# Second layer's routing cut into small pieces between the mixer's steps, with fixed regions per expert in the sorted rows

## The chip, the cores and the metric

One NeuronCore of a Trainium2 chip runs one program. Its engines are TensorE (PE in the profile), VectorE (DVE), ScalarE (ACT), GpSimd (POOL) and SyncE (SP), which issues most of the DMAs. The metric is the device time of one execution in microseconds, less is better.

## The reference, cut to what matters

Two transformer-like layers work on x of 4 groups (batch entries) of 512 rows of 256 features. Layer 0 is an attention and a mixture of 16 experts (top 2), layer 1 a state-space mixer and a mixture of 32 experts (top 6) with a shared expert. The change touches the mixer and the second mixture:

```
h = _layernorm(x, axis=-1) * (1 + cb) + sb
x = x + gb * _L1_ffn_ref(h, ...)
# _L1_ffn_ref, HID = 256, N_EXP = 32, F_EXP = 96, TOP_K = 6, F_SH = 192
scores = jax.nn.sigmoid(x @ gate_w)
topk_w, topk_i = jax.lax.top_k(scores, TOP_K)
topk_w = topk_w / (jnp.sum(topk_w, axis=-1, keepdims=True) + 1e-20)
combine = jnp.sum(jax.nn.one_hot(topk_i, N_EXP, dtype=topk_w.dtype) * topk_w[..., None], axis=1)
g = jnp.einsum('td,edf->tef', x, wg)
u = jnp.einsum('td,edf->tef', x, wu)
act = jax.nn.silu(g) * u
routed = jnp.einsum('tef,efd,te->td', act, wd, combine)
shared = jax.nn.silu(hidden_states @ sg) * (hidden_states @ su) @ sd
return routed + shared
```

The mixer (`ssm_forward`) works on each group alone, so a group's x is final for the second mixture as soon as the mixer has finished that group.

## The kernel before, in words

The program runs four stages in order: attention, `experts(0)`, the mixer, `experts(1)`. Between stages all engines meet (`together`).

**The mixer.** After a start part it runs a stream of steps, 32 per group (`FT`), one for each pair of heads, software-pipelined over five steps (`tiles[0]` to `tiles[4]` in `mixer_pe_step`, `mixer_act_step`, `mixer_dve_step`, `mixer_pool_step`). `mixer_stream` writes four steps of a group out in line, then `between` (the tail of the group before: its rows are scaled, gated and added to x), then a hardware loop (`Fori`) of seven turns of four steps. Each engine executes its part of a step in written order and waits on the others by semaphores. PE: projection of x (L1752), transposes (L1766), the products of a chunk (L1775, L1780), projection of the gate (L1752), chunk states (L1792, L1799), output projection (L1806). DVE: states `st` (L1887, L1892), `m_mat` (L1939, into `outs`), `xdt` (L1904), three conv taps `cv` (L1914), `yd`, `xc`, `sgt` (L1921 to L1933). POOL: `xdec` (L1966), a sum of squares (L1974), `yg` (L1981). SP loads `wi`, `l_mat`, `wo`, 1.1 MB in each step.

**The second mixture** (`experts(1)`). Rows are handled in 16 tiles of 128 (`NT`). First comes the routing of all 16 at once: DVE takes the statistics of the layer norm (L1146), normalizes (L1159), PE turns (L949), ACT modulates into `ht`, PE makes the logits (L959), ACT and DVE the sigmoid (L1080, L1177, L1178), DVE the top 8 and their indices (L1181, L1185), the one-hot tables `eqs` (L1190) and their sum `mask` (L1194). PE counts, with a triangular matrix, each row's rank within its expert, and each expert's rows. DVE then knows how many tiles of 128 each expert takes (L1207 to L1217), adds the expert's first row and picks for each row and choice the place in `sorted_rows` (L1219 to L1221). POOL scatters the rows there by 96 indirect DMAs of 128 rows (L1134), each row with its weight and its destination in two further words (L1128, L1129). SP has meanwhile loaded the weights (L920 to L925) and waits for all scatters before it loads the first sorted tile (L931).

Then 143 units run in a pipeline: 16 units of the shared expert, which read `ht` and need no scatter, and 127 tiles of `sorted_rows` (`Q1`). A unit is: turn (L997), gate and up product (L1007 or L1013, the expert's number read from `te` into a register, L1010), tanh (L1099), silu (L1229, L1234), turn (L1023 to L1026), down product (L1038 or L1042), scaling (L1106), and an indirect DMA of 128 rows into `chosen_rows` (L1138). Eight tile buffers (`xt`): a load waits for the put of the tile eight before. At the end SP loads the chosen rows group by group (L937), and PE and DVE add the six.

## Time and profile before

| | us |
|---|---|
| median of 3 runs | 2503.9 (2501.62 to 2505.82) |
| the profiled execution | 2514.42 |
| its span | 2512.6 |
| mean granted PE clock | 0.889 of full |
| busy: PE, DVE, ACT, POOL | 2006.3, 1661.3, 1451.7, 901.4 |

Everything below is read on the profiled execution's axis, from 0 to 2512.6. The stages: attention to 629.6, the first mixture to 862.6, the mixer's start to 988, its stream to 2044 and its last tail to 2051.2, then the second mixture: routing, scatters and shared units to 2243.7, routed units to 2461.7, the adding of the chosen rows to the end. A line number such as L1134 is one of the kernel before. Times of a row are its start and its duration; the bracket at its end is how long its engine had been idle and what released it ("remote" and "issue" mean that no instruction of another engine in the profile explains the end of the wait).

### The profile page before, as it was taken

To read this page: it belongs to the slowest core of one execution; us is meant where nothing else is said; L and a number is where in the kernel's file an instruction comes from. 1 tells how busy PE (TensorE), PEld (TensorE's weight loads), DVE (VectorE), ACT (ScalarE), POOL (GpSimd) and SP (SyncE) were. 2 spreads that over 40 slices of the span, in tenths; PEclk is the share of its full clock that TensorE was granted. 3 is DMA by queue.
4 is the path that set the end of the run, shared out by engine and by line. 5 is a ranking of instruction groups with operands and counts; after the bars stand their busy time and mean duration, and the time that the engine had idled before them with its cause. 6 is when DMAs were issued, how large, how long until landed. Compare 5 with 4: busy or idle time off the path is not lost.

```text
span 2512.6 us, 45894 instructions
## 1 busy us (share of the span) xinstructions
PE 2006.3 (80%) x12171; PEld 1623.7 (65%) x12171; DVE 1661.3 (66%) x3638; ACT 1451.7 (58%) x3953; POOL 901.4 (36%) x832
## 2 busy tenths in 40 slices
PE   4786858777369446999999999999999975259995
PEld 4565646666347244888878887888788863147772
DVE  4665746566424577888888888888888866034444
ACT  1463726456124155888878888888888851015551
POOL 0120302011243110444444444444444434745551
PEclk8796969779679778999999999999999987579998
DMA  3160582011433302444434443444344434225556
GB/s 121 43 192 8 166 229 101 34 67 64 191 98 108 143 5 85 141 150 144 150 121 150 147 148 126 144 150 150 124 143 148 150 104 123 101 90 157 157 154 259
DMA packets 155925, 319.51 MB, mean 127 GB/s; under 512 B 20177, under 2 KB 93905, under 8 KB 153489
## 3 DMA queue, kind: packets, MB, share of 16 engines
q1 hardware_dynamic: 141296, 278.31, 34.7%
q0 software_dynamic: 14496, 39.73, 4.4%
q8 instruction: 47, 0.77, 0.1%
q14 instruction: 86, 0.70, 0.1%
HBM read 231.68 MB, written 86.29 MB: 127 GB/s over the span
## 4 chain that ended last, share of the span: by engine, by line
PE 60%; DVE 12%; issue 10%; ACT 9%; DMA 2%; POOL 2%; PEldq 1%; SPq 1%; DVEq 1%; ACTq 1%; PEld 1%; POOLq 0%
PE bank L1752 14%; PE bank L1806 8%; PE bank L1013 6%; PE bank L1780 5%; ACT work L669 4%; PE bank L1042 3%; PE bank L1799 3%; PE bank L1792 3%; PE bank L1766 3%; DVE nmax L589 2%; PE bank L1775 2%; PE bank L997 1%; PE bank L741 1%; PEldq L142 1%; POOL sorted_rows L1134 1%
## 5 line engine op out<-in xcount | busy, mean ns | idle before, releaser
L1752 PE MATMUL bank<-h_hi,wi 128*128 128x512 f32 x1024 | 402.1, 434 | 0.9 <-ACTq L142 0.9
L1914 DVE SCALAR_TENSOR_TENSOR cv<-bank,cw,cv 128x511 f32<-128x511 f32 (+2 forms) x384 | 287.4, 748 | 83.6 <-ACT cv L1847 50.6
L1841 ACT ACTIVATE l_mat<-l_mat,cum_tok 128x128 f32<-128x128 f32 x1024 | 315.7, 429 | 0.0
L1966 POOL TENSOR_TENSOR xdec<-xdt,dec_tok 128x384 f32<-128x384 f32 x128 | 107.8, 842 | 464.4 <-DVE xdt L1904 464.4
L1981 POOL TENSOR_TENSOR yg<-yd,sgt 128x512 f32<-128x512 f32 x128 | 228.2, 1783 | 76.1 <-DVE yd L1921 76.1
L1806 PE MATMUL bank<-wo,yg 128*128 128x256 f32 x1024 | 242.4, 380 | 0.3 <-POOL yg L1981 0.3
L1138 POOL DMA_INDIRECT chosen_rows<-experts_yo,experts_xt x174 | 167.7, 964 | 192.3 <-ACT experts_yo L1106 169.8
L1229 DVE SCALAR_TENSOR_TENSOR experts_sg<-experts_th,bank 128x96 f32<-128x96 f32 (+2 forms) x190 | 53.8, 283 | 274.8 <-ACT experts_th L1099 206.4
L1752 PEld LDWEIGHTS bank<-h_hi,wi 128*128 128x128 f32 x1024 | 194.4, 190 | 62.2 <-issue 24.2
L1752 PE MATMUL bank<-h_lo,wi 128*128 128x512 f32 x512 | 202.9, 396 | 0.0
L1099 ACT ACTIVATE experts_th<-bank 128x96 f32<-128x96 f32 (+2 forms) x190 | 52.0, 273 | 256.9 <-remote 116.8
L1806 PEld LDWEIGHTS bank<-wo,yg 128*128 128x128 f32 x1024 | 184.9, 191 | 20.5 <-POOL yg L1981 0.7
L1974 POOL TENSOR_TENSOR gates<-gates,sq 128x512 f32<-128x512 f32 x128 | 163.2, 1275 | 92.4 <-ACT sq L1857 92.4
L1013 PE MATMUL bank<-experts_wgu,experts_xT 128*128 x696 | 177.6, 378 | 8.4 <-issue 5.8
L808 POOL CAST w_hi<-w_raw 128x512 fp32r<-128x512 f32 x32 | 19.5, 610 | 452.1 <-ACTq L142 314.8
L1862 ACT ACTIVATE thx<-cv 128x512 f32<-128x512 f32 x128 | 80.7, 631 | 166.9 <-DVE cv L1914 166.9
L1832 ACT ACTIVATE y_off<-bank,e_tok 128x64 f32<-128x64 f32 x768 | 170.1, 327 | 6.1 <-PE bank L1799 6.1
L669 ACT ACTIVATE work<-bank,nmax 128x512 f32<-128x512 f32 (+3 forms) x256 | 135.1, 535 | 65.0 <-DVE nmax L589 65.0
L1939 DVE TENSOR_TENSOR outs<-l_mat,g_mat 128x1024 f32<-128x1024 f32 x128 | 156.6, 1224 | 0.0
L589 DVE TENSOR_REDUCE nmax<-bank 128x1 f32<-128x512 f32 (+3 forms) x256 | 117.5, 483 | 57.9 <-PE bank L746 57.9
L627 DVE TENSOR_TENSOR hb<-bank,pt_hi 128x512 fp32r<-128x512 f32 (+1 forms) x192 | 114.4, 599 | 47.2 <-ACT pt_hi L622 47.1
L1134 POOL DMA_INDIRECT sorted_rows<-experts_rows,slot_u x128 | 125.3, 979 | 55.7 <-issue 36.1
(296 smaller groups left out, 4898.8 us busy)
## 6 DMA issues: line engine op xcount, KB each, us to landing
wi<-in_weights_split SPq DMA_DIRECT2D x128, 512.0 KB, 3.4
l_mat<-running_sums SPq DMA_DIRECT2D x128, 512.0 KB, 4.5
experts_xt<-sorted_rows SPq DMA_DIRECT2D x174, 129.0 KB
experts_got<-chosen_rows SPq DMA_DIRECT2D x32, 512.0 KB, 9.9
wo<-out_weights_normed SPq DMA_DIRECT2D x128, 128.0 KB, 2.0
sorted_rows<-blank SPq DMA_DIRECT2D x5, 2709.0 KB, 26.7
w_raw<-in_wi SPq DMA_DIRECT2D x32, 256.0 KB, 2.6
in_weights_split<-w_hi SPq DMA_DIRECT2D x32, 256.0 KB, 2.8
```

The costliest lines, as they stand in the source:

```text
L589: last = e.tensor_reduce(nmax[:, h, q:q + 1], bank[n % 3][:, col:col + P * (q + 1)], AX.X, ALU.max, negate=True)
L669: last = e.activation(pp[:, h % 2, QOFF[q]:QOFF[q] + w], bank[u][:, col:col + w], ACT.Exp, bias=nmax[:, h, q:q + 1], accum_out=ssum[:, h, ...
L1013: mm = e.matmul(B_G[n % 2][:, 0:2 * F], xT[:, q % TURNED, k, :], wgu[:, bass.ds(owners[q], 1), k, :], start=(k == 0), stop=(k == KD - 1))
L1138: e.indirect_dma_start(chosen[layer], bass.IndirectOffsetOnAxis(xt[:, q % LOADED, D + 1:D + 2].bitcast(U32), 0), yo[:, q % YIELDED, :], No ...
L1752: mm = e.matmul(dst[:, :], l, r[:, k, tok], start=(n == 0), stop=(n == 3 * KD - 1))
L1806: mm = e.matmul(token_major((bank[0], bank[1]), i), yg[:, w.two, i * P:(i + 1) * P], wo[:, w.two, :], start=False, stop=w.end, skip_group_ ...
L1832: last = e.activation(y_off[:, c, rows], PO[:, c * P + hh * SSM_P:c * P + (hh + 1) * SSM_P], ACT.Identity, scale=e_tok[:, c, hh, bass.ds(w ...
L1841: last = e.activation(part, part, ACT.Relu, bias=cum_tok[:, c, hh, bass.ds(w.g, 1)], scale=-1.0)
L1914: e.scalar_tensor_tensor(out=cv[:, w.two, n:SEQ], in0=PSX[w.two][:, 0:SEQ - n], scalar=cw[:, bass.ds(w.f, 1), TAPS - 1 - n], in1=cv[:, w.t ...
L1939: v.e.tensor_tensor(m_mat[:, w.two, :, :], l_mat[:, w.four, :, :], g_mat[:, w.b, :, :].rearrange("p c l -> p (c l)").unsqueeze(1).broadcas ...
L1974: e.tensor_tensor(sq_sum[:, w.b % 2, :], sq_sum[:, w.b % 2, :], sq[:, :], ALU.add).then_inc(s_acc, 1)
L1981: e.tensor_tensor(yg[:, w.two, :], yd[:, :], sgt[:, w.four, :], ALU.mult).then_inc(s_yg, 1)
```

## The change

**Routing by group.** The routing of a group of four tiles is cut into pieces, numbered by a step s from 0 to 11 and a place in it. `mixer_stream` gives the pieces of group b-1 to the twelve steps after the group's tail, which are now written out in line (`ROUTED = 3` turns of four) on every engine. DVE's pieces stand at the head ("a") or the end ("z") of its part of the step, PE's before L1792 and L1799 ("m", "p"), ACT's at the head or in the middle, POOL's at the end. The later steps stay a hardware loop on all engines but POOL, which has them in line too and issues 24 scatters for the group there: two in each of four steps, one in each of twelve, and four in the next group's first steps. The rows that are scattered are made by POOL from the normalized rows and a modulation row that SP loads (`mod_row`), and are kept in `freed_rows` and, for the shared units, in DRAM (`h_rows`). Groups 0 to 2 are routed so. The last group's twelve steps run at the start of the second mixture with nothing between them, and its 24 scatters after them.

**Fixed regions.** Expert k now has rows from k*17*128 in `sorted_rows`, so a place is known without the other groups' counts; `taken` carries the counts from group to group. The unused rows of an expert's last tile are written when all counts are known, by 32 copies of 128 rows from DRAM to DRAM (`blank_tiles`), which replace the blanking of all of `sorted_rows`. A tile's number is read into a register before its load (`tile_at`), as the expert's number is on PE.

**Order on SP's queue** in the second mixture: modulation row, first eight shared tiles, weights, the last group's `h_rows`, the 32 copies, the other eight shared tiles, and, when scatters and copies have landed, the routed tiles. Shared units are turned and read like routed ones. `got` has three buffers instead of four.

```
-    xs = [nc.dram_tensor(f"sorted_rows{l}", (q * P, ROW), FP32).ap() for l, q in enumerate((Q0, Q1))]
+    xs = [nc.dram_tensor(f"sorted_rows{l}", (q * P, ROW), FP32).ap() for l, q in enumerate((Q0, (DEEP + 1) * E1))]
+    blank_tiles = nc.dram_tensor("blank_tiles", (E1 * P, ROW), FP32).ap()
+    mod_rows = nc.dram_tensor("modulation_rows", (GROUPS, 2 * D), FP32).ap()
+    h_rows = nc.dram_tensor("modulated_rows", (NT * P, D), FP32).ap()
...
+        def blank_after():
+            e.wait_ge(s_blanked, 2)
+            past = xs[1][DEEP * E1 * P:, :]
+            for to, sets in ((blank_tiles, slice(0, E1)), (past, slice(E1, SETS))):
+                tiles = to.rearrange("(q p) c -> p q c", p=P)
+                e.dma_start(tiles[:, :, 0:D + 1],
+                            blank[:, 0:1, 0:D + 1].broadcast_to([P, E1, D + 1])).then_inc(s_blank[1], 16)
...
-                blank_rows(1, Q1)
+                blank_after()
...
+    def load_mod_row(e, r):
...
+        e.dma_start(mod_row[:, :, :].rearrange("p c n -> p (c n)"),
+                    mod_rows[r:r + 1, :].broadcast_to([P, 2 * D])).then_inc(s_modrow, 16)
+
+    def route_sync(en, r, s, at):
+        if (s, at) == (1, "a"):
+            load_mod_row(en.e, r)
+        if (s, at) == (6, "a"):
+            keep_rows(en.e, r)
+
+    def keep_rows(e, r):
+        e.wait_ge(*q_rowed(r + 1))
+        for n in range(2):
+            first = (r * TT + 2 * n) * P
+            e.dma_start(h_rows[first:first + 2 * P, :].rearrange("(i p) d -> p i d", p=P),
+                        freed_rows[n][:, :, r, 0:D]).then_inc(s_hrows, 16)
...
+        if 1 <= s <= 4 and at in "mp":
+            n = 2 * (s - 1) + "mp".index(at)
+            if n == 0:
+                e.wait_ge(*q_rows(r + 1))
+            i, k = n // KD, n % KD
+            e.transpose(turned_at(r, n), xn[:, i, k * P:(k + 1) * P], ident[:, :]).then_inc(q_turned.sem, 1)
+        if (s, at) == (5, "p"):
...
+        if (s, at) == (9, "m"):
+            e.wait_ge(*routed(MASKED, r))
...
+        if (s, at) == (0, "m"):
+            e.wait_ge(*q_var(r + 1))
+            e.activation(rs[:, 1, 0:TT], rs[:, 0, 0:TT], ACT.Sqrt).then_inc(q_root.sem, 1)
...
+        if 2 <= s <= 5 and at == "a":
...
+            e.wait_ge(*q_turned(KD * TT * r + n + 1))
+            e.activation(h32[:, k, i * P:(i + 1) * P], turned_at(r, n), ACT.Identity, bias=shift,
...
+        if (s, at) == (0, "a"):
+            for i in range(TT):
+                v.own.add(e.bn_stats(stats[:, i, :], x[:, r * TT + i, :]))
+            e.wait_ge(s_dve, v.own.now())
...
+        if (s, at) == (1, "a"):
+            for i in range(TT):
+                last = e.tensor_scalar(xn[:, i, :], x[:, r * TT + i, :], mv[:, i, 0:1], rs[:, 2, i:i + 1],
+                                       ALU.subtract, ALU.mult)
+            last.then_inc(q_rows.sem, 1)
+        if 2 <= s <= 5 and at == "a":
...
+        if (s, at) == (6, "z"):
+            e.wait_ge(*routed(SQUASHED, r))
+            v.step(e.tensor_scalar(scores, scores, 1.0, None, ALU.add))
+            v.step(e.reciprocal(scores, scores))
+        if (s, at) == (7, "a"):
+            for i in range(TT):
+                v.own.add(e.max(top[:, r * TT + i, :], scores[:, i, :]))
...
+        if (s, at) == (7, "z"):
+            e.wait_ge(*q_rowed(r + 1))
+            for i in range(TT):
...
+        if s == 8:
+            for i in ((0, 1), (2, 3))[at == "z"]:
+                v.own.add(e.tensor_reduce(chosen_by[:, i, :], by_tile[:, i, :, :].rearrange("p j e -> p e j"), AX.X,
...
+        if (s, at) == (9, "a"):
+            v.step(e.tensor_reduce(taken_f[:, :], chosen_by.rearrange("p i e -> p e i"), AX.X, ALU.add))
+            v.own.add(e.tensor_tensor(taken[:, r + 1, :], taken[:, r, :], taken_f[:, :], ALU.add))
...
+        if (s, at) == (10, "a"):
+            e.wait_ge(*routed(RANKED, r))
...
+        if (s, at) == (10, "z"):
...
+        if (s, at) == (11, "a"):
+            v.step(e.tensor_reduce(slots_f, equal, AX.X, ALU.add))
...
+                    e.wait_ge(*q_scat[i](16 * TOP1 * r))
...
+    def route_pool(q, r, s, at):
+        e = q.e
+        if (s, at) == (2, "z"):
+            e.wait_ge(*q_rows(r + 1))
+            e.wait_ge(s_modrow, 16 * (r + 1))
...
+    def route_scatter(q, r, n):
+        e = q.e
+        j, i = n // TT, n % TT
+        if i == 0 and j == 0:
...
+                e.wait_ge(s_blank[1], BLANK[1])
+        if j:
+            e.wait_ge(*q_scat[i](16 * (TOP1 * r + j)))
+        row = row_of(r, i)
+        e.tensor_copy(row[:, D:D + 1], tw[:, r * TT + i, j:j + 1])
+        e.tensor_copy(row[:, D + 1:D + 2].bitcast(I32), tok[:, j, r * TT + i:r * TT + i + 1]).then_inc(q_meta.sem, 1)
+        e.wait_ge(*q_meta(r * (TOP1 * TT + 1) + j * TT + i + 2))
+        e.indirect_dma_start(xs[1], bass.IndirectOffsetOnAxis(slot_g[:, i, j:j + 1], 0), row, None).then_inc(q_scat[i].sem, 16)
...
+        for b in range(GROUPS + 1):
             for u in range(U):
                 run(b, 0, u)
+                if scatter and b >= 2:
+                    scatter(en, b - 2, TOP1 * TT - U + u)
...
-            with en.e.Fori(1, FT // U) as it:
-                for u in range(U):
-                    run(b, it, u)
...
+            if b == GROUPS:
+                break
+            if b:
+                for it in range(1, 1 + ROUTED):
+                    for u in range(U):
+                        run(b, it, u, routing(b - 1, (it - 1) * U + u))
+            first = 1 + (ROUTED if b else 0)
+            if scatter and b:
+                for it in range(first, FT // U):
+                    for u in range(U):
+                        run(b, it, u)
+                        n = (it - first) * U + u
+                        for m in range(n + min(n, U), n + 1 + min(n + 1, U)):
+                            scatter(en, b - 1, m)
+            else:
+                with en.e.Fori(first, FT // U) as it:
+                    for u in range(U):
...
         if w.live:
             e.wait_ge(s_ss, done(w.g))
+            route("a")
...
+        route("z")
...
             e.wait_ge(s_o, done(w.g - 2))
             e.tensor_tensor(yg[:, w.two, :], yd[:, :], sgt[:, w.four, :], ALU.mult).then_inc(s_yg, 1)
+        route("z")
...
+                    e.dma_start(xt[:, n % LOADED, 0:D], h_rows[n * P:(n + 1) * P, :]).then_inc(s_xt[n % LOADED].sem, 16)
+                else:
+                    at = e.value_load(tile_at[0:1, n - SH:n - SH + 1], min_val=0, max_val=(DEEP + 1) * NE - 1)
+                    e.dma_start(xt[:, n % LOADED, :], xs[layer].rearrange("(q p) c -> q p c", p=P)[bass.ds(at, 1), :, :]
+                                .rearrange("o p c -> p (o c)")).then_inc(s_xt[n % LOADED].sem, 16)
+
+            load_mod_row(e, GROUPS - 1)
+            e.wait_ge(s_hrows, 16 * 2 * (GROUPS - 1))
+            for n in range(LOADED):
+                load(n)
...
+                e.dma_start(sdn[:, :, :], io["sdn"]).then_inc(s_w.sem, 16)
+            for c in range(WLOADS):
+                part = slice(c * NE // WLOADS, (c + 1) * NE // WLOADS)
+                e.dma_start(wgu[:, part, :, :], io[f"wgu{layer}"][:, part, :, :]).then_inc(s_w.sem, 16)
+                e.dma_start(wd[:, part, :, :], io[f"wd{layer}"][:, part, :, :]).then_inc(s_w.sem, 16)
+            keep_rows(e, GROUPS - 1)
+            e.wait_ge(*BLANKS)
+            for k in range(NE):
+                at = e.value_load(blank_at[0:1, k:k + 1], min_val=0, max_val=DEEP * NE * P - P)
+                e.dma_start(xs[layer][bass.ds(at, P), :], blank_tiles[k * P:(k + 1) * P, :]).then_inc(s_blank[0], 16)
+            e.wait_ge(s_hrows, 16 * 2 * GROUPS)
+            for n in range(LOADED, SH):
+                load(n)
+            e.wait_ge(*LOADS_AT)
+            for i in range(TT):
+                e.wait_ge(*q_scat[i](16 * TOP * GROUPS))
...
+            for n in range(SH, UNITS_ALL):
+                load(n)
...
+        def pool(g):
+            e = g.e
+            for step in range(ROUTED * U):
+                route_pool(g, GROUPS - 1, step, "z")
+            for n in range(TOP * TT):
+                route_scatter(g, GROUPS - 1, n)
```

DVE around two of the written-out steps; `st` to `sgt` is the mixer's own part of a step, and `wsum`, `tw`, `freed_rows` (here the ranks' places) and `xn` (here the one-hot tables) belong to the routing. Before, one in-line step:

```order
L1887 COPY st<-bank6 128x128
L1892 SCALAR_TENSOR_TENSOR st<-st,e_in,bank6 128x64 x4
L1939 TENSOR_TENSOR outs<-l_mat,g_mat 128x1024
L1904 TENSOR_TENSOR xdt<-bank6,dt_tok 128x512
L1914 SCALAR_TENSOR_TENSOR cv<-bank4,cw,cv 128x511
L1914 SCALAR_TENSOR_TENSOR cv<-bank4,cw,cv 128x510
L1914 SCALAR_TENSOR_TENSOR cv<-bank4,cw,cv 128x509
L1921 SCALAR_TENSOR_TENSOR yd<-xc,dsk,bank7 128x512
L1927 SCALAR_TENSOR_TENSOR xc<-thx,cv 128x512
L1933 SCALAR_TENSOR_TENSOR sgt<-thg,bank2 128x512
```

Now, the seam between steps 9 and 10:

```order
L2209 SCALAR_TENSOR_TENSOR xc<-thx,cv 128x512
L2215 SCALAR_TENSOR_TENSOR sgt<-thg,bank2 128x512
L1558 TENSOR_REDUCE wsum<-top 128x4
L1559 TENSOR_SCALAR wsum<-wsum 128x4
L1560 RECIPROCAL wsum<-wsum 128x4
L1561 TENSOR_SCALAR wsum<-wsum 128x4
L1562 TENSOR_TENSOR tw<-top,wsum 128x32
L1566 TENSOR_TENSOR freed_rows0<-base_row,bank6 128x128
L2169 COPY st<-bank6 128x128
L2174 SCALAR_TENSOR_TENSOR st<-st,e_in,bank6 128x64 x4
```

Six instructions stand between `sgt` of one step and `st` of the next, where there was none.

POOL in a step of the mixer that carries scatters (`yg` is its last own instruction of a step, `xdec` its first). Before:

```order
L1966 TENSOR_TENSOR xdec<-xdt,dec_tok 128x384
L1974 TENSOR_TENSOR gates<-gates,sq 128x512
L1981 TENSOR_TENSOR yg<-yd,sgt 128x512
L1966 TENSOR_TENSOR xdec<-xdt,dec_tok 128x384
L1974 TENSOR_TENSOR gates<-gates,sq 128x512
```

Now:

```order
L2264 TENSOR_TENSOR yg<-yd,sgt 128x512
L1608 COPY freed_rows<-tw 128x1
L1609 COPY freed_rows<-tok 128x1
L1611 DMA sorted_rows<-freed_rows,slot_u 73728x258
L1608 COPY freed_rows<-tw 128x1
L1609 COPY freed_rows<-tok 128x1
L1611 DMA sorted_rows<-freed_rows,slot_u 73728x258
L2249 TENSOR_TENSOR xdec<-xdt,dec_tok 128x384
```

Two scatters with their four small copies stand between `yg` and the next `xdec`.

SP in the second mixture, from the weights on. Before:

```order
L924 DMA experts_wgu<-in_wgu 128x3072
L925 DMA experts_wd<-in_wd 96x2048
L931 DMA experts_xt<-sorted_rows 128x258 x127
L937 DMA experts_got<-chosen_rows 128x1024 x24
```

Now (the four rows from `TENSOR_LOAD blank_at` stand 32 times, once for each expert):

```order
L2388 DMA experts_wgu<-in_wgu 128x3072
L2389 DMA experts_wd<-in_wd 96x2048
L1452 DMA modulated_rows<-freed_rows 128x2x256 x2
L2393 TENSOR_LOAD blank_at
L2393 ISA x2
L2394 ISA
L2394 DMA sorted_rows<-blank_tiles 16x2064
```

The copies stand on the queue ahead of the second half of the shared tiles.

## Rows read from the trace of the kernel before

**Rows 1.** Busy time by stretch: length, PE, PEld, DVE, ACT, POOL, PE clock, DMA share, GB/s.

```profile
988.00:2044.00 1056.00, 1030.96 (x7030) 853.78 (x7030) 911.46 (x1689) 875.33 (x2432) 499.48 (x386) 0.99 0.43 139
2051.20:2243.70 192.50, 76.71 (x317) 52.91 (x318) 67.02 (x221) 19.07 (x37) 98.37 (x120) 0.67 0.40 124
2243.70:2461.70 218.00, 205.16 (x1150) 167.21 (x1149) 93.03 (x389) 126.80 (x379) 120.97 (x126) 1.00 0.50 148
```

**Rows 2.** The same view of one looped step and one in-line step.

```profile
1154.59:1162.63 8.04, 8.03 (x57) 6.63 (x56) 7.06 (x14) 6.78 (x20) 3.90 (x3) 1.00 0.44 140
1242.68:1250.50 7.82, 7.82 (x57) 6.71 (x56) 7.14 (x15) 6.90 (x21) 3.94 (x4) 1.00 0.48 144
```

**Rows 3.** Timeline: where POOL and DVE stand idle in a mixer step.

```profile
1151.43 0.84 POOL L1966 TENSOR_TENSOR xdec<-xdt,dec_tok 128x384 f32<-128x384 f32 x1 [2.82 <-DVE xdt L1904]
1247.41 2.31 DVE L1914 SCALAR_TENSOR_TENSOR cv<-bank,cw,cv 128x511 f32<-128x511 f32 x3 [0.45 <-ACT cv L1847]
```

**Rows 4.** Timeline: DVE in the routing of all 16 tiles.

```profile
2051.43 5.32 DVE L1146 BATCH_NORM_STATS2 stats<-x 128x6 f32<-128x256 f32 x16 [0.36 <-DVEq L142]
2058.85 0.18 DVE L225 TENSOR_TENSOR rs<-rs 128x16 f32<-128x16 f32 x1
2059.69 1.38 DVE L1159 TENSOR_SCALAR xn<-x,mv,rs 128x256 f32<-128x256 f32 x4
2075.29 3.35 DVE L1178 RECIPROCAL h<-h 128x512 f32<-128x512 f32 x1
2078.79 1.59 DVE L1181 MAX8 top<-h 128x8 f32<-128x32 f32 x16
2080.60 0.18 DVE L1185 FIND_INDEX8 top_i<-top,h 128x8 uint32<-128x32 f32 x1
2096.95 0.68 DVE L1219 TENSOR_TENSOR outs<-experts_eqs,h 128x512 f32<-128x512 bf16 x1
2097.67 0.69 DVE L1220 TENSOR_REDUCE slot_f<-outs 128x16 f32<-128x512 f32 x1
```

**Rows 5.** Timeline: PE, the logits of four tiles.

```profile
2067.88 1.87 PE L959 MATMUL bank<-gwf,experts_ht 128*128 128x32 f32 x16
```

**Rows 6.** Timeline: POOL's scatters, and a DVE instruction with two SBUF inputs beside them.

```profile
2103.23 0.68 DVE L1219 TENSOR_TENSOR outs<-experts_eqs,h 128x512 f32<-128x512 bf16 x1
2103.54 1.22 POOL L1134 DMA_INDIRECT sorted_rows<-experts_rows,slot_u  x1 [0.30 <-DVE slot_u L1221]
...
2131.25 0.21 POOL L1128 COPY experts_rows<-tw 128x8 f32<-128x8 f32 x1
...
2131.87 0.98 POOL L1134 DMA_INDIRECT sorted_rows<-experts_rows,slot_u  x1 [0.28 <-issue]
```

**Rows 7.** Timeline and stretches: from the first weight load to the first routed unit.

```profile
2051.25 0.33 SPq L920 DMA_DIRECT2D experts_sgu<-in_sgu  x1
2085.00:2090.00 5.00, 0.45 (x2) 0.18 (x3) 4.76 (x12) 0.00 (x0) 0.00 (x0) 0.50 0.74 161
2098.80 5.08 PE L1007 MATMUL bank<-experts_sgu,experts_ht 128*128 128x384 f32 x8 [1.13 <-DVE te L1224]
2243.68 0.82 PE L1013 MATMUL bank<-experts_wgu,experts_xT 128*128 x4
```

**Rows 8.** Timeline: two shared units in a row that also turn a tile.

```profile
2238.49 1.46 PE L1007 MATMUL bank<-experts_sgu,experts_ht 128*128 128x384 f32 x4
...
2241.08 1.46 PE L1007 MATMUL bank<-experts_sgu,experts_ht 128*128 128x384 f32 x4
```

**Rows 9.** Line view and waits: reading a register, and PE waiting for a tile.

```profile
L1010 PEldq TENSOR_LOAD <-te x174: 295/301/536, 713.8 to 2457.3; - x174
...
PEld bank L997 <- DMA experts_xt<-sorted_rows: 4.6, 7, 1.3
```

**Rows 10.** Timeline: a PE product and its DVE reader while POOL scatters back to back.

```profile
2189.34 0.42 PE L1024 MATMUL bank<-ident,experts_act 128*128 128x128 f32 x1
...
2214.78 0.42 DVE L1242 COPY experts_aT<-bank 128x256 f32<-128x256 f32 x1 [15.00 <-issue]
```

491 lines of the change are left out of this document (456 added, 35 removed).

## The prediction, as it was put on record

> **What bounds the kernel now.** I read the busy times by stretch first [rows 1]. The mixer's stream takes 1056 us with PE busy 98% of it at full clock and DVE 86%. The second mixture takes 192.5 us until its first routed unit with PE busy 40%, and POOL busy 98 us; then 218 us of routed units with PE at 94%. So there are two kinds of stretch: one where every engine is nearly full, and one that mostly waits. The change moves work from the second into the first, and the question is what a piece costs in each.
>
> The stretch that waits, first. SP starts the weights at 2051.25, they fill the DMA engines until about 2089 (the stretch 2085 to 2090 is the first that is not full), PE starts shared units at 2098.80, and the first routed product stands at 2243.68 [rows 7]. Shared units need 2.6 us each where nothing is in their way (2238.49 to 2241.08) [rows 8], 16 of them 42 us. The rest is the wait for 96 scatters at 1.27 us and more (a scatter of 0.98 and 0.3 of issue [rows 6]), some 134 us from 2099 on. The scatters end last here.
>
> Then a mixer step. In the loop a step takes 8.04 us, written in line 7.82, and PE is busy all of it in both [rows 2]. DVE comes next: in the in-line step it stands still 0.45 us once, for ACT's `cv` [rows 3], so its own part fills about 7.4 of 7.82. POOL has a hole of 2.82 us between `yg` and the next `xdec` [rows 3].
>
> **The change part by part.**
>
> *DVE's routing pieces in the mixer.* Of 16 tiles four go to each group. Statistics 5.32/4 = 1.3 and their aggregates, estimated at 0.3; normalized rows 1.38; sigmoid's reciprocal 3.35/4 = 0.8; maxima 1.59/4 = 0.4; four index searches with their loads at about 0.17, 0.7 [rows 4]. An instruction over 512 elements takes 0.68 or 0.69 [rows 4]; scaled down to 192 elements with the 0.15 that a small one costs anyway, 0.28. Of such there are four comparisons, four products, four reductions and four evictions of 128 columns: 16 x 0.28 = 4.5. One reduction of 768 is 1.0. Some 18 small ones at 0.2 (0.18 and the gap [rows 4]) are 3.6. Sum 14.0, call it 14.2 with the waits between.
>
> *What of that lies on the path.* Steps 2 to 5 carry only an eviction each on DVE (1.1 of the 14.2), which its spare 0.42 takes. There PE is the bound, with two small transposes in each and the logits in step 5, 1.87 [rows 5]: together 2.6. The other eight steps carry 13.1 on DVE, of which the spare takes 8 x 0.42 = 3.4: 9.7. All twelve steps are now in line, which gives back 12 x 0.22 = 2.6 [rows 2]. Net 9.7 a group, and there are three: **+29**. From below, 7 a group, since after a tail DVE waits for PE anyway. From above, 18, if no spare is used, every hand-over between engines costs something, and PE's clock stays low for longer behind the tail.
>
> *ACT and SP in the mixer.* ACT's root needs two table loads, in step 0 only, where DVE's own piece of 2 us delays the reader as much; at nothing, covered by that piece, and at 1 us a group if it were not. SP runs steps ahead; its waits for the tail and for POOL's rows end before PE needs the loads behind them. At nothing.
>
> *POOL in the mixer.* A scatter with its copies takes 1.6 us (2131.25 to 2132.85) [rows 6]. One fits the hole of 2.82. Two, 3.2, miss it by 0.4 in four steps of a group, and `xdec` is read about 0.9 after it is due. The four copies of rows (two in steps 2 and 3) are 2.5 to 3.6 and hardly miss. At nothing; priced below as rivals.
>
> *The start of the second mixture.* The last group's routing is a chain through the same pieces without cover: 14 us of DVE, 5 of PE and ACT, some hand-overs, so about 21 us, and the tables of tiles 6 us later, at +27 counted from 2051.2. POOL's 24 scatters at 1.6 run from +21 to +60 and land by +63. The weights, 9.9 MB in 38 us before, get 1.3 MB of tiles and modulation ahead and about 14 scatters (1.8 MB) beside them: +51. PE's first shared unit starts there. Sixteen at 2.6, 3 for a low clock at first and 2 until the first routed product: +97.6. In between stands SP: it issues the 32 copies from +26 on, each with a register read of 0.30 [rows 9], its arithmetic and an issue of 0.33 and more, about 1.1 together, so until +61, and their 4.2 MB lie on the queue behind the weights and before shared tile 8. I put tile 8 at +75; PE wants it at +70. With that 5 us the first routed product stands at +102, where it was at +192.5: **-90**. Bounds: -97 with no stall, -75 if the copies go at half of the weights' rate.
>
> *Routed units.* A tile's load now reads a register first, 0.5 us more in a ring of eight buffers: 0.06 a unit, 8 us over 127 if the ring bounds everywhere. PE waited for a tile only 7 times, 4.6 us in all [rows 9], while SP was always waiting for puts. **+4**, between 0 and 9. Three `got` buffers instead of four: **+1**, between 0 and 3; the loads of the fourth group wait for the first's sum, behind transfers still under way.
>
> *The blanking and small transfers in the attention stage* have room behind a weight stream that waits there; at nothing.
>
> **Sum.** 29 - 90 + 4 + 1 = -56. On the profiled execution that is 2514.4 to 2458; it stands 10.5 above the median of the runs, and I take the difference over: 2503.9 - 56 = **2448**. The forecast's own range runs from 21 - 97 = -76 (2428) to 54 - 75 + 9 + 3 = -9 (2495), with most of it between 2430 and 2475.
>
> **The rivals.**
>
> *A, the pieces cost twice* (12%): DVE's pieces stand before `st`, on which PE's transposes wait at once, so PE stands still in every such step, and if its clock drops for it, a step loses more than the piece. About 20 us a group, +60 in all: 2479. For it: PE and DVE are both near full [rows 2]. Against it: gaps of 1 to 3 us are short.
>
> *B, the queue decides* (10%): copies and tile 8 land at about +95, then 8 units follow: first routed product at +125, -67: 2471. For it: all these transfers share SP's queue.
>
> *C, the pieces are nearly free* (8%): DVE catches up in the looped steps and only PE's 2.6 counts. +10 in all: 2429.
>
> *D, late signals, slower than before* (4%). While POOL scatters back to back, a product that PE finished at 2189.8 is read by DVE at 2214.78 [rows 10], though DVE was idle; this grows with the length of the scatters and ends with them. If a scatter in a mixer step makes PE's signals late there, each of the 60 steps that carry one pays. At 1.5 us a step that is +90: 2538. It ends slower than before from 0.93 us a step on (56/60). Against it: scatters in the routed units, one in 1.7 us, leave PE at 94% [rows 1], and in the mixer it is one in 8.
>
> *E, the shared port* (3%). POOL's scatter took 1.22 beside a DVE instruction with two SBUF inputs and 0.98 alone, and the DVE instruction 0.68 in both cases [rows 4, 6]: here POOL paid. If DVE paid instead, with the full 0.98 for each of the 72 scatters in the mixer, it would be +70: 2518, slower than before.
> The Trainium skill, "SBUF — State Buffer", section "SBUF: two separate sides", says that the shared port pair is locked exclusively for a whole instruction by whichever of the two starts first, a DVE instruction with two SBUF inputs counting against a GpSimd one that reads SBUF. By that rule DVE should pay about as often as POOL; the rows above show only POOL paying.
>
> *F, it does not do what it says* (3%): the scatters of groups 0 to 2 slip out of the mixer, because one of them waits for its places or its predecessor, and the second mixture waits for them as before. About no change, 2500.
>
> **How the numbers follow.** The forecast has 60%, the rivals the rest. The range that leaves out no more than 2 in 10: below, C and the forecast's low end, 2426; above, A, B and most of the forecast, 2486. A measurement of this kernel can tell 0.2%, 5 us, from no change. Faster by more: the forecast, A, B, C, 90%; within: most of F and a little of the forecast's upper end, 3%; slower: D and E, 7%.
>
> **What would show it.** In the profile after: an in-line step that carries a piece of 1 us on DVE should take about 8.5 to 9 us and a group some 10 us longer than 264; POOL's scatters in the mixer should last 1.0 to 1.3, with `xdec` on time; PE's first shared unit should stand near +51 and its first routed product near +102 from the stage's start; the pitch of routed units should be 1.72 to 1.78. The prediction is wrong if mixer steps that carry only a scatter grow beyond 8.3 us (D, E), if PE stands still before shared unit 8 for more than 15 us (B), or if the first shared unit does not start before the weights have landed and they take longer than to +60.

## The result, and the profile after

| | before | changed |
|---|---|---|
| median | 2504.84 us | 2470.73 us (2465.92 to 2480.99, 4 runs) |
| ratio | 1 | 0.9874, 95% interval 0.9854 to 0.9894 |
| the profiled execution, its span | 2514.42, 2512.6 | 2465.92, 2464.1 |

The changed kernel is 34 us faster, inside the range (2426 to 2486) and in the forecast direction, but 22 us short of the 56 that I forecast (the prediction counted from the median of three runs of before, 2503.9; a fourth makes it 2504.84). Two rows cut each profile into stages: the four tails of the mixer (DVE's addition to x, first and last start) and the second mixture's puts (POOL, first and last start). Columns: count, shortest, median and longest duration in ns, first and last start in us. Of the kernel before:

```profile
L1957 DVE TENSOR_TENSOR x<-x,gates x4: 1224/1224/1226, 1265.7 to 2049.8; 128x1024 f32<-128x1024 f32 x4
L1138 POOL DMA_INDIRECT chosen_rows<-experts_yo,experts_xt x127: 963/967/977, 2249.5 to 2462.9; - x127
```

Of the changed kernel, with PE's first shared and first routed product from its timeline:

```profile
L2240 DVE TENSOR_TENSOR x<-x,gates x4: 1224/1224/1225, 1260.0 to 2075.9; 128x1024 f32<-128x1024 f32 x4
...
2123.52 2.93 PE L2449 MATMUL bank<-experts_sgu,experts_xT 128*128 128x384 f32 x4
...
2176.07 0.82 PE L2454 MATMUL bank<-experts_wgu,experts_xT 128*128 x4
...
L2551 POOL DMA_INDIRECT chosen_rows<-experts_yo,experts_xt x127: 966/967/977, 2181.9 to 2414.9; - x127
```

| stretch | before | changed | difference | forecast |
|---|---|---|---|---|
| to the first tail | 1265.7 | 1260.0 | -5.7 | 0 |
| first to last tail, three groups | 784.1 | 815.9 | +31.8 | +29 |
| last tail to first routed product | 193.9 | 100.2 | -93.7 | -90 |
| first routed product to last put | 219.2 | 238.8 | +19.6 | +4 |
| last put to the end | 49.7 | 49.2 | -0.5 | +1 |

A put is the indirect DMA that writes a finished tile to `chosen_rows`. One term is wrong, the routed units, by some 16 us. The table's sum is -48.5 where the medians differ by 34.1. Two of its lines are flattered by the execution that was profiled before. The stretch to the first tail moves with the same code: in another profile of the changed kernel (label e10_after_again) the tails run from 1269.1, 9 us later. And in experiment 3 below, the kernel before with an edit that acts only in the routed units, the last tail starts at 2049.3 and the first routed product at 2235.2: 185.9, not 193.9. With 186 for before, and the first line at nothing, the sum is 31.8 - 85.8 + 19.6 - 0.5 = -34.9, near the difference of the medians. So the start gained 86 to 94 us. Why the same code took 185.9 in one execution and 193.9 in the other is open. Against the forecast the routed units then account for 16 of the 22 us, start and mixer for 4 and 3, and the end gives 1 to 2 back.

The same views as [rows 1] and [rows 2], of the changed kernel: length, then busy time of PE, PEld, DVE, ACT and POOL, PE clock, DMA share, GB/s. First the stretches (mixer's stream, start of the second mixture, routed units), then steps of the second group that carry the logits, nothing, the sigmoid's end and the maxima and indices, the comparisons and sums, and two scatters.

```profile
988.00:2070.00 1082.00, 1031.12 (x7101) 857.24 (x7099) 956.25 (x1859) 888.29 (x2452) 612.72 (x610) 0.99 0.46 146
2077.10:2176.10 99.00, 53.40 (x225) 38.54 (x226) 45.73 (x148) 16.82 (x42) 36.10 (x76) 0.69 0.72 217
2176.10:2414.90 238.80, 212.87 (x1151) 167.98 (x1149) 92.88 (x389) 129.29 (x380) 121.93 (x126) 1.00 0.47 136
...
1303.91:1313.53 9.62, 9.62 (x74) 8.50 (x72) 8.91 (x18) 7.50 (x21) 5.45 (x4) 1.00 0.67 227
1313.53:1321.36 7.83, 7.83 (x58) 6.71 (x57) 5.62 (x11) 6.71 (x20) 2.34 (x4) 1.00 0.44 155
1321.36:1331.91 10.55, 8.01 (x57) 6.63 (x56) 10.20 (x29) 6.94 (x20) 4.02 (x4) 1.00 0.35 112
1331.91:1341.56 9.65, 8.00 (x57) 6.63 (x56) 9.43 (x20) 6.88 (x20) 3.88 (x4) 1.00 0.40 124
1384.67:1392.83 8.16, 8.14 (x58) 6.56 (x56) 7.23 (x14) 6.88 (x20) 6.85 (x9) 1.00 0.57 195
```

A step without a piece takes 7.83 as before. Where DVE carries 3.2 us of pieces PE waits 2.5 for `st` (`2.54 <-DVE st` below), and its clock stays at 1.00, the full 2.4 GHz. Two scatters, one with a copy that took 0.60, lie between `yg` and `xdec`, and the step is hardly longer than a looped one (8.16 against 8.04 [rows 2]). In experiment 8 below, where every engine has these steps in line, a step with two scatters takes 7.83, as one without (the row is of experiment 8):

```profile
1374.83:1382.66 7.83, 7.83 (x58) 6.71 (x57) 7.18 (x14) 6.91 (x20) 6.62 (x10) 1.00 0.54 181
```

Of the changed kernel, PE's wait for `st`, and POOL in the step with two scatters:

```profile
1327.17 0.63 PE L2043 MATMUL bank<-ident,xc 128*128 128x128 f32 x4 [2.54 <-DVE st L2174]
...
1387.44 1.03 POOL L1611 DMA_INDIRECT sorted_rows<-freed_rows,slot_u  x1 [0.28 <-POOL freed_rows L1609]
1388.47 0.60 POOL L1608 COPY freed_rows<-tw 128x1 f32<-128x1 f32 x1
...
1389.47 0.98 POOL L1611 DMA_INDIRECT sorted_rows<-freed_rows,slot_u  x1 [0.28 <-POOL freed_rows L1609]
1390.48 0.85 POOL L2249 TENSOR_TENSOR xdec<-xdt,dec_tok 128x384 f32<-128x384 f32 x1
```

### The profile page after: what moved, and what is told of

Same layout as the page of the kernel before. It is cut to its first block, busy times and chain, and to the rows that moved or that the text cites. A ratio compares the mean times of both kernels' runs of the same rounds, so it can differ in the third digit from the quotient of the medians.

```text
span 2464.1 us, 45422 instructions
## 1 busy us (share of the span) xinstructions
PE 1991.0 (81%) x12166; PEld 1613.9 (65%) x12166; DVE 1690.0 (69%) x3745; ACT 1468.5 (60%) x3985; POOL 955.3 (39%) x1016
## 4 chain that ended last, share of the span: by engine, by line
PE 54%; DVE 16%; ACT 10%; issue 7%; DMA 6%; SPq 2%; POOL 2%; PEldq 1%; DVEq 1%; ACTq 1%; PEld 1%; POOLq 0%
PE bank L2029 13%; PE bank L2085 7%; PE bank L2057 5%; ACT work L697 5%; PE bank L2070 3%; PE bank L2078 3%; PE bank L2043 3%; PE bank L1044 2%; PE bank L2454 2%; DMA chosen_rows<-experts_yo,experts_xt 2%; DVE nmax L617 2%; DMA experts_xt<-sorted_rows 2%; DVE cv L2196 2%; PE bank L1073 2%; PE bank L2052 1%
## 5 line engine op out<-in xcount | busy, mean ns | idle before, releaser
L2551 POOL DMA_INDIRECT chosen_rows<-experts_yo,experts_xt x127 | 122.9, 968 | 146.2 <-ACT experts_yo L2531 145.6
L2584 DVE SCALAR_TENSOR_TENSOR experts_sg<-experts_th,bank 128x96 f32<-128x96 f32 (+1 forms) x143 | 38.0, 266 | 180.3 <-ACT experts_th L2524 180.2
L2057 PE MATMUL bank<-outs,xdt 128*64 128x128 f32 x2048 | 142.5, 282 | 0.0
L2174 DVE SCALAR_TENSOR_TENSOR st<-st,e_in,bank 128x64 f32<-128x64 f32 x512 | 121.0, 278 | 26.4 <-DVE st L2169 11.7
L2132 ACT ACTIVATE l_mat<-l_mat 128x1024 f32<-128x1024 f32 x128 | 137.9, 1078 | 0.0
```

The costliest lines, as they stand in the source:

```text
L2057: mm = e.matmul(PY[rows, c * P:(c + 1) * P], xdt[:, w.four, c, rows], m_mat[:, w.two, hh, c * P:(c + 1) * P], start=False, stop=(c == NC - 1),
L2132: e.activation(l_mat[:, w.four, :, :], l_mat[:, w.four, :, :], ACT.Exp, scale=-1.0).then_inc(s_l, 1)
```

## The experiments

**Where the routed units lost 20 us.** My theory after the result: the ring of eight tile buffers sets the pace, and the register read stands in it. The pitch is the mean time from the start of one put to the start of the next. A buffer of the ring goes round as put (POOL), load (SP), turn (PE), and, in the order in which the program is written, three units later the next put. If that is all, eight units take the ring's fixed part plus three units, and what is added to the fixed part is shared by 8 - 3 = 5 units, not by 8 as in the prediction. The three is read off the program; in the trace of before, a tile's put starts 7.7 us after its turn starts (mean of the last 107 tiles), 4.5 pitches, a part of which does not grow with the pitch. The rival: the fixed regions, or an address out of a register, make the tiles' traffic slower. The next rows show the read on SP's queue in the changed kernel, 127 times, and from the start of a put to the issue of the load that waited for it, one pair of before and one of the changed kernel, each near the shortest that occurs:

```profile
L2375 SPq TENSOR_LOAD <-te_of_loads x127: 262/268/713, 2150.6 to 2405.0; - x127
L2375 SPq FUSED_REGOPS  x127: 152/152/159, 2150.9 to 2405.3; - x127
...
2303.04 0.97 POOL L1138 DMA_INDIRECT chosen_rows<-experts_yo,experts_xt  x1 [0.79 <-ACT experts_yo L1106]
2305.47 0.32 SPq L931 DMA_DIRECT2D experts_xt<-sorted_rows  x1
...
2263.11 0.97 POOL L2551 DMA_INDIRECT chosen_rows<-experts_yo,experts_xt  x1 [1.09 <-ACT experts_yo L2531]
2266.27 0.34 SPq L2376 DMA_DIRECT2D experts_xt<-sorted_rows  x1
```

2.43 before, 3.16 now: 0.73 more, of which the read with its arithmetic is 0.56 and the address of the DMA the rest. A fifth of 0.73 is 0.146; the pitch of puts, from the rows of the puts above, went from 213.4/126 = 1.694 to 233.0/126 = 1.849, 0.155 more.

*Experiment 1*, the read ahead of the wait:

```
+                if n >= SH:
+                    at = e.value_load(tile_at[0:1, n - SH:n - SH + 1], ...)
                 if n >= LOADED:
                     ...put(e, n - LOADED - SH)
...
-                    at = e.value_load(tile_at[0:1, n - SH:n - SH + 1], ...)
```

> The changed kernel with one edit: SP reads a tile's number into its register before it waits for the put that frees the buffer, not behind that wait. Theory (the read stands in the ring of eight buffers, and as a tile's own unit takes three units from turn to put, what is added to the ring is shared by 8 - 3 = 5 units): put to load falls from 3.62 us to about 2.95, the pitch of puts from 1.849 to 1.70 to 1.73, the kernel 15 to 18 us shorter than the changed one, about 2454. By my prediction's arithmetic (0.5 us over 8 units) only 8 us come back, about 2463. Rival (the fixed regions or the computed address itself make the tiles' traffic slower): pitch stays at 1.85, about 2471.

*Experiment 2*, four reads behind the wait:

> The changed kernel with three further reads of the same register behind the wait of each tile's load. Each is 0.56 us in SP's order, 1.69 together. Shared by 5 units: the pitch rises by 0.34 to about 2.19, +43 us, about 2514. Shared by 8: by 0.21 to 2.06, +27 us. If the ring did not bound: no change of the pitch.

*Experiment 3*, a read in the kernel before:

```
                 if q >= LOADED:
                     put(e, q - LOADED)
+                    if layer == 1:
+                        e.value_load(te[0:1, q:q + 1], min_val=0, max_val=NE - 1)
```

> The kernel before with one register read behind the wait of each tile's load in the second mixture; its value is not used, so addresses and regions stay as they were. Theory (read in the ring, shared by 5): 0.56 us more from put to load, the pitch of puts 1.694 to about 1.80, +14 us on the stretch of routed units. Shared by 8: 1.76, +9. Rival (fixed regions): pitch stays at 1.69 to 1.70.

*Experiment 4*, `LOADED` 10 instead of 8, on top of experiment 1:

> The changed kernel with the read before the wait and ten tile buffers instead of eight. Theory (the ring bounds, not PE): with 10 - 3 = 7 units to share, the ring no longer bounds; the pitch falls to PE's own pace where it waits for nothing, 1.5 to 1.62, about 13 to 28 us less than the 8-buffer version with the read moved: 2428 to 2442. Rival (PE and its hand-overs with ACT and DVE bound by then): pitch stays near 1.70, no gain over the 8-buffer version.

The puts of the four, in this order:

```profile
L2552 POOL DMA_INDIRECT chosen_rows<-experts_yo,experts_xt x127: 963/967/979, 2188.4 to 2410.4; - x127
...
L2553 POOL DMA_INDIRECT chosen_rows<-experts_yo,experts_xt x127: 967/968/979, 2180.0 to 2542.2; - x127
...
L1140 POOL DMA_INDIRECT chosen_rows<-experts_yo,experts_xt x127: 964/968/977, 2241.1 to 2473.7; - x127
...
L2553 POOL DMA_INDIRECT chosen_rows<-experts_yo,experts_xt x127: 963/967/977, 2177.2 to 2383.8; - x127
```

| | pitch of puts | time, ratio to before |
|---|---|---|
| changed kernel | 1.849 | 2470.7, 0.987 (0.985 to 0.989) |
| 1, read ahead of the wait | 1.762 | 2458.6, 0.982 (0.980 to 0.985) |
| 2, four reads | 2.875 | 2591.9, one execution |
| 3, before with a read | 1.846 | 2523.5, one execution (before beside it 2501.6) |
| 4, ring of ten | 1.640 | 2435.6, 0.974 (0.972 to 0.976) |

Experiment 3 decides between theory and rival. Addresses and regions are those of before, a read is added, and the pitch rises by 0.152 to that of the changed kernel. The rival falls: beside the read, the regions cost nothing that these profiles can tell (the pitch of this ring moved between 1.835 and 1.880 over seven profiles of kernels that leave it alone).

In experiment 1 the mean time from put to load (the same 107 tiles) fell from 3.61 to 3.02 us, as asked (2.95), but the pitch fell by only 0.087 of 0.155, less than the theory asked (1.70 to 1.73), and the kernel gained 12 us instead of 15 to 18. The address of the DMA, 0.15 us, stays in the ring.

How the addition is shared is not settled. Of 0.56 us added, experiment 3 shows 0.152 in the pitch, 0.27 of it; the changed kernel 0.155 of 0.73, 0.21; experiment 1 took 0.56 out and gave back 0.087, 0.16. A fifth lies in their middle, and an eighth below all three, but with the spread above and one profile each, no single share is shown.

The waits for a tile follow the pitch. Before, changed, experiment 1 and experiment 3, over the stretch of routed units (total us, times, longest):

```profile
PEld bank L997 <- DMA experts_xt<-sorted_rows: 4.6, 7, 1.3
...
PEld bank L2438 <- DMA experts_xt<-sorted_rows: 15.4, 21, 1.6
...
PEld bank L2439 <- DMA experts_xt<-sorted_rows: 7.6, 11, 1.6
...
PEld bank L999 <- DMA experts_xt<-sorted_rows: 18.6, 28, 2.2
```

Experiment 4 takes the ring out of the way: no wait of PE for a tile is left in this view, and it is busy 204.5 of 208.1 us between its first and last routed product, where with eight buffers (experiment 1) it was 207.9 of 223.5. The pitch, 1.640, is just above the 1.5 to 1.62 that I expected, the time within its range. SP still waits for puts, 91 times and 71.2 us here, 86 times and 100.2 us in the changed kernel:

```profile
SPq L2378 <- DMA chosen_rows<-experts_yo,experts_xt: 71.2, 91, 12.2
```

PE's busy time in experiment 4, and in experiment 1:

```profile
2171.40:2379.50 208.10, 204.51 (x1142) 168.00 (x1141) 91.98 (x386) 125.05 (x376) 119.01 (x123) 1.00 0.50 153
...
2182.60:2406.10 223.50, 207.91 (x1142) 168.80 (x1141) 92.03 (x385) 126.26 (x376) 119.00 (x124) 0.99 0.48 144
```

Experiment 2 missed both numbers. Four reads of 0.56 each and the DMA take some 2.8 us of SP's own time for a tile, so SP itself became the bound (2.875), and the dose was too large to tell five from eight. Two reads would have been the better dose.

Experiment 4 gained at the start too, which I had not looked for: with ten tiles loaded ahead instead of eight, the wait before a shared tile is 0.15 us instead of 7.56, and the first routed product stands 91.3 us after the last tail (2171.4 - 2080.1) instead of 98 to 100.

```profile
2152.98 0.44 PE L2440 MATMUL bank<-ident,experts_xt 128*128 128x128 f32 x2 [0.15 <-DMA experts_xt<-modulated_rows]
```

**The start of the second mixture.** SP's side and the unit that waited, in the changed kernel:

```profile
2104.22 42.10 SPq L2394 DMA_DIRECT2D sorted_rows<-blank_tiles  x32
2146.42 3.90 SPq L2373 DMA_DIRECT2D experts_xt<-modulated_rows  x8
...
2149.65 0.69 PE L2438 MATMUL bank<-ident,experts_xt 128*128 128x128 f32 x2 [7.56 <-DMA experts_xt<-modulated_rows]
```

The 32 copies take SP 1.32 us each, and shared tile 8 is loaded behind them. Four orders were tried.

*Experiment 5*: the two loads of the shared expert's weights raise a semaphore of their own, PE waits for that alone, and for the others before the first routed unit.

> The changed kernel, but PE waits for the shared expert's two weight loads alone before the shared units, and for all weights before the first routed unit. Theory (two things stand ahead of shared tile 8: the weights and SP's 32 copies, and the copies end last): the first shared unit starts some 19 us earlier, at about 29 us after the last tail instead of 48; PE then waits longer before tile 8, and the first routed product hardly moves, within 3 us of 100.2 after the tail. Rival (the weights are what binds): the first routed product comes 15 to 19 us earlier.

*Experiment 6*, in the loop over the copies, and no loads behind it:

```
+                if k == 14:
+                    e.wait_ge(s_hrows, 16 * 2 * GROUPS)
+                if k >= 14 and (k - 14) % 2 == 0 and LOADED + (k - 14) // 2 < SH:
+                    load(LOADED + (k - 14) // 2)
```

> The changed kernel with the loads of shared tiles 8 to 15 between SP's copies, one after every second copy from the fifteenth on, instead of behind all 32. Theory: the wait of 7.56 us before shared unit 8 goes, and with it the slow clock behind it; the first routed product stands at about 90 after the last tail instead of 100.2. If the copies' transfers on the same queue held tile 8 up (rival B of the prediction), the wait would stay.

*Experiment 7*, both, with 1 for 14:

> Both edits: PE starts the shared units on their own weights, and tiles 8 to 15 are loaded amid the copies from the second copy on. Theory: the first shared unit at about 29 after the last tail, 16 units of 2.6 and some waiting for weights that are still landing; the first routed product at 78 to 84 after the tail, near where copies and scatters end, instead of 100.2: 16 to 22 us less than the changed kernel, about 2450. If transfers of the weights hold tile 8 up, it is 90 or more.

*Experiment 9*, as 7, but tiles 8 to 11 without the wait for the last group's rows, tiles 12 to 15 and the wait from the twenty-first copy on:

> As the kernel with both orders, but SP no longer waits for the last group's rows in DRAM before shared tile 8: tiles 8 to 11, which are of the third group, are loaded after the second, fourth, sixth and eighth copy, and only before tile 12, at the twenty-first copy, does SP wait for the rows. Theory (in the kernel with both orders SP stood from 2110.17 to 2130.15 for rows whose transfers were behind the weights, and that pushed the copies' end back by 20 us): no such stand; the copies end about 48 us after SP's first, the first sorted tile is loaded at about 79 after the last tail, the first routed product at 82 to 86, against 103.9 there and 100.2 in the changed kernel. Rival (the transfers of the weights or scatters hold the tiles anyway): 95 or more.

| | last tail | first shared | first routed | tail to routed | time |
|---|---|---|---|---|---|
| changed kernel, two profiles | 2075.9, 2084.5 | 2123.5, 2133.2 | 2176.1, 2182.9 | 100.2, 98.4 | 2470.7, 2469.4 (medians) |
| 5 | 2082.5 | 2112.8 | 2180.8 | 98.3 | 2473.2, one execution |
| 6 | 2080.6 | 2132.5 | 2176.1 | 95.5 | 2464.7, one execution |
| 7 | 2079.9 | 2110.1 | 2183.8 | 103.9 | 2474.0, ratio 0.983 |
| 9 | 2083.2 | 2113.5 | 2174.0 | 90.8 | 2463.5, one execution |

Experiment 5 came out as said: PE starts 18 us sooner, then waits 24.08 before tile 8 instead of 7.56, and the end stays.

```profile
2155.70 0.69 PE L2439 MATMUL bank<-ident,experts_xt 128*128 128x128 f32 x2 [24.08 <-DMA experts_xt<-modulated_rows]
```

In experiment 6 the wait before tile 8 is gone (three waits of 0.72, 0.35 and 0.22 us stand in its place), and from the first shared to the first routed product it takes 43.6 us against 52.6 and 49.7. But its first shared product stood 51.9 us after the tail, against 47.6 and 48.7, so that the start gained 3 to 5 us, not 10. In the runs that leave this part alone that product came 47.6 to 51.0 after the tail; whether the edit delayed it is open.

The forecast for experiment 7 was wrong: its start is slower than that of the changed kernel, and it took 2474.0, not 2450. Its SP stands 20 us behind its second copy, and PE pays at the end, before the first sorted tile (the first row is the write of the last group's rows):

```profile
2092.56 2.66 SPq L1452 DMA_DIRECT2D modulated_rows<-freed_rows  x2
2108.22 1.95 SPq L2395 DMA_DIRECT2D sorted_rows<-blank_tiles  x2
2130.15 0.35 SPq L2374 DMA_DIRECT2D experts_xt<-modulated_rows  x1
...
2178.78 0.69 PE L2440 MATMUL bank<-ident,experts_xt 128*128 128x128 f32 x2 [20.79 <-DMA experts_xt<-sorted_rows]
```

SP waited there for the last group's rows to be in DRAM. They were issued behind the weights on the same queue, at 2092.56. For the changed kernel the trace has the landings: issued at 2088.56 and 2088.98, the two writes landed at 2122.26 and 2125.60, the last weights at 2122.30. Experiment 9 takes that stand away, but gains 8 to 9 us where I expected 14 to 18: the copies still end SP's work only at 2164.4, 52.9 us after the first instead of 48. One pair of copies took 6.39 us while weights were landing, where most pairs took 1.8 to 2.1 (the second row shows the last five, at 1.1 each):

```profile
2119.01 6.39 SPq L2397 DMA_DIRECT2D sorted_rows<-blank_tiles  x2
...
2158.81 5.62 SPq L2397 DMA_DIRECT2D sorted_rows<-blank_tiles  x5
```

**The loop in the mixer.** *Experiment 8*:

```
-                with en.e.Fori(first, FT // U) as it:
+                for it in range(first, FT // U):
                     for u in range(U):
                         run(b, it, u)
```

> The changed kernel with the mixer's remaining hardware loops on PE, DVE, ACT and SP written out in line. Theory (a step costs 8.05 looped and 7.82 in line, the term by which I gave back 2.6 us a group): 27 steps of the first group and 16 of each other, 75 in all, at 0.23 each, 17 us less than the changed kernel, about 2453. Rival (fetching so much more code costs what the loop costs): no gain.

2455.0, ratio 0.974 (0.972 to 0.976). The tails and a stretch of the first group:

```profile
L2240 DVE TENSOR_TENSOR x<-x,gates x4: 1224/1225/1226, 1258.2 to 2062.9; 128x1024 f32<-128x1024 f32 x4
...
1130.00:1250.00 120.00, 120.00 (x849) 102.92 (x846) 109.95 (x199) 105.28 (x289) 60.53 (x47) 1.00 0.44 147
```

From first to last tail 804.7 against 815.9: 11.2 us over 48 steps, 0.23 each, as in [rows 2]. PE is busy 120.00 of 120 us, and the rival, that fetching the code costs what the loop costs, falls. Before took 2520.7 beside it, more than in the other series, so the ratio flatters it. The stages do not: from the first output projection to the last tail it takes 17.5 us less than the changed kernel (1054.7 to 1072.2), as said.

**All together.** *Experiment 10*, the changed kernel again, and *experiment 11*, experiments 4, 8 and 9 in one:

> The changed kernel unedited, beside the next one on the same chip: ratio to before 0.984 to 0.990, with the stages as in its first profile within 3 us, but for the attention stage, which moved by 6 us from run to run with the same code.

> All that the experiments found, together: registers read before the wait and a ring of ten tiles (together -35 us by the ratios), the mixer in line (-17.5), and the new order at the start of the second mixture (-15 to -18). If they add up, 66 to 71 us less than the changed kernel beside it, a ratio to before of about 0.960. If they share a cover (the ring's gain shortens only what the puts allow, code fetching in line delays SP), less: 0.965 to 0.970.

On one chip 2469.4 (ratio 0.986, 0.983 to 0.989) and 2420.5 (0.968, 0.964 to 0.972): 49 us, not 66 to 71. The changed kernel repeated itself: its first ratio was 0.987, and of its stages only the routed units moved by more than the 3 us allowed (242.3 against 238.8). In the kernel with all of it, mixer and routed units gave what they gave alone (first to last tail 815.4 to 804.5; first routed product to last put 242.3 to 212.6). The start gave 4 us (98.4 to 94.8), since SP's copies again end last.

I had counted the start twice. The 35 us of experiment 4 held 7 to 9 us of the start already, from the ten tiles loaded ahead: it stood at 91.3 there without the new order. With the new order on top it stands at 94.8. PE's first shared product comes 20 us sooner, but SP's 32 copies, with loads among them, take 57 us from first to last instead of 42, and PE waits 3.6, 8.5 and 5.0 us for tiles. So for a ring of ten these profiles show no gain from the order of experiment 9; experiments 4 (35) and 8 (17.5) alone add up to more than the 49 us measured. *Experiment 12* takes every second copy to ACT's queue, in its first sixteen steps of shared units:

> The kernel with all that was found, but ACT issues every second of the 32 copies, one in each of its first sixteen steps of shared units, and SP the other sixteen; SP loads tiles 12 to 15 behind its copies. Theory (SP's own time for 32 copies, 1.3 to 1.6 us each, is what ends last before the first sorted tile): SP is through some 45 to 55 us after the last tail instead of 85, the scatters end last, and the first routed product stands at 76 to 82 after the tail instead of 94.8: 13 to 19 us less, a ratio to before of 0.961 to 0.963. Rival (ACT's copies delay its hand-overs to PE, 1.3 us in each shared unit): the shared units take 3.5 us or more each and the first routed product stays at 90 or more.

```profile
2099.30 21.97 SPq L2368 DMA_DIRECT2D sorted_rows<-blank_tiles  x13
2121.37 2.13 SPq L2381 DMA_DIRECT2D experts_xt<-modulated_rows  x4
...
2135.67 0.98 POOL L1611 DMA_INDIRECT sorted_rows<-freed_rows,slot_u  x1 [0.28 <-POOL freed_rows L1609]
...
2139.94 59.80 SPq L2383 DMA_DIRECT2D experts_xt<-sorted_rows  x38
2142.18 0.69 PE L2446 MATMUL bank<-ident,experts_xt 128*128 128x128 f32 x2 [5.19 <-DMA experts_xt<-sorted_rows]
```

2412.8, ratio 0.964 (0.959 to 0.968), forecast 0.961 to 0.963. The medians of experiments 11 and 12, on two chips, are 7.7 us apart and their intervals overlap; the start gained the 13 that the forecast allowed at the least. Last tail 2064.8, first routed product 2146.6: 81.8 after it. SP is through at 2123.5, 58.7 after the tail where I said 45 to 55, and now the last scatter (2135.67) ends last. That it was the copies on SP's queue is shown by this run; the shared units kept their 2.6 us with ACT's copies among them.

## Why the prediction was right and where it failed

**The mixer, +29, measured 31.8.** Right by its own steps: the pieces' length on DVE (911.5 to 956.3 us busy in the stream, 14.9 a group where I said 14.2) less its spare, PE's transposes and logits, the in-line gain (which experiment 8 measured alone at 0.23 a step). A step with a piece of 3.2 us grew by 2.7, and one that carries nothing stayed at 7.83. Rival A (pieces cost twice) needed PE's clock to fall in such waits; it did not. D and E had said that scatters hurt the mixer: steps with two of them took 8.16, and 7.83 in line (experiment 8), and POOL's scatters 0.98 to 1.04.

By the rule that the prediction weighed (the Trainium skill, "SBUF — State Buffer", "SBUF: two separate sides") DVE should pay beside POOL's scatters wherever the scatter starts first. In the changed kernel 54 of DVE's products `outs`, with two SBUF inputs, start while a scatter runs, most of them 0.30 us into its 1.03. They took 1.22 us in the mean and 1.30 at most, against 1.22 alone, so here the trace does not agree. Beside POOL's own arithmetic, where it makes the rows to be scattered, both sides do pay: six products took 1.42 instead of 1.22, and POOL's second product 2.26 instead of 1.29.

```profile
1419.73 1.02 POOL L1611 DMA_INDIRECT sorted_rows<-freed_rows,slot_u  x1 [0.28 <-POOL freed_rows L1609]
1420.03 1.22 DVE L2222 TENSOR_TENSOR outs<-l_mat,g_mat 128x1024 f32<-128x1024 f32 x1
...
1297.53 3.51 POOL L1593 TENSOR_TENSOR freed_rows<-freed_rows,gates 128x512 f32<-128x512 f32 x2
1298.48 1.42 DVE L2222 TENSOR_TENSOR outs<-l_mat,g_mat 128x1024 f32<-128x1024 f32 x1
```

**The start, -90, measured 86 to 94.** Right in its sum, and in its terms within 8 us. The first routed product stood at 98.9 from the tail's end where I said 102, the first shared unit at 46.4 (51), and PE stood 7.56 us before tile 8 (5). The copies took SP until 69 (61): 1.32 us each, not 1.1. The bound of -97 without a stall is a slip; its own terms, +97.6 against +192.5, give -95. Rival B, whose mark was a stand of over 15 us, did not come, though experiment 5 shows that it was near: without the wait for all weights PE would have stood 24.

**The routed units, +4, measured +19.6: the step that failed.** I divided by the ring's eight buffers, 0.5 us by 8, and took off again for the 7 times that PE had waited. Three things were wrong. The read with its address is 0.73 in the ring, not 0.5. The share of it that a unit pays is more than an eighth in all three comparisons, 0.16 to 0.27; a fifth, from a ring that holds three units of the pitch itself, gives 0.146 x 126 = 18.4 of the 19.6 measured, but experiments 1 and 3 fall on either side of it. And the 7 waits [rows 9] were no sign that the ring had room to spare: units took 1.694 where PE, once the ring was wide, took 1.640 (experiment 4), and with the read PE waited 21 times, 15.4 us in all. That SP was always waiting for puts said nothing either way: in the ring of ten it waits as often, and PE never.

**Three `got` buffers, +1, measured -0.5:** nothing that can be seen.

## What to carry to other kernels

What is put between "buffer free" and "load issued" in a ring of n buffers can cost more per unit than 1/n of itself, since a part of the round grows with the pitch; here 0.16 to 0.27 of it with n = 8. If the round contains k steps of the pipeline, 1/(n - k) is a first estimate, which these runs bear out only roughly. Whether the ring has room is not to be seen from the issuing engine, which waits for the free buffer either way, but from how often the reader waits for its tile. If it does, read the register before the wait or add a buffer; adding two was worth more here (pitch 1.762 to 1.640) than moving the read (1.849 to 1.762). When a stage starts on one queue, list for each reader what stands ahead of its data on that queue: moving one wait alone (experiment 5) gains nothing where another wait ends last, and moving it in front of other work (experiment 7) can lose. And before gains are added up, ask which stage each comes from: the wider ring and the new order shortened the same start. A piece put into a nearly full engine cost the piece less that engine's spare, and no more.

## What the hardware showed that I had not expected

- A read of a register on SP holds its queue for 0.56 us (0.27 for the load, 0.15 for arithmetic, and gaps), and a DMA with a computed address 0.15 more; four in a row bound a stream of tiles at 2.875 us.
- A mixer written out in line is 0.23 us a step faster than in a loop of four steps, and PE was busy 120.00 of 120 us in the stretch shown, with no sign of waits for code there.
- The late signals of [rows 10] did not come back. With 24 scatters, and with pauses among them, behind the mixer, shared units kept their 2.6 us while the last scatters ran (to 2146.8 in the changed kernel). What makes them late was not tried.
- The kernel before took a median of 2501.6 to 2504.8 us in four series of runs and 2520.7 in a fifth (beside experiments 5 to 8), where the stages of the changed kernels were as in the others. Why is open; this is why experiments 5 to 8 are compared by stages.
